# One kernel, two layers, one core: loading the weights in two groups and finishing three of the derived weights inside the main program

## The reference, cut to what matters

```
x_norm = layernorm(x) * norm_g + norm_b
x_proj, z = split(x_norm @ in_proj_W)            # 384 channels each
y_fwd, y_bwd = light_s6(windows of x_proj)       # xproj_W, dt_W, dt_b, A_log, D; 4 steps, 8 states
y_dw  = depthwise 3 x 3 convolution of x_proj    # dw_kernel
y     = alpha * (y_fwd + y_bwd) / 2 + (1 - alpha) * gelu(y_dw @ pw_W)     # alpha = sigmoid(gate)
x_out = x + (y * silu(z)) @ out_W
x     = x_out + gelu((layernorm(x_out) * norm2_g + norm2_b) @ fuse_W1 + fuse_b1) @ fuse_W2 + fuse_b2
```

## Time and profile before

| what | us |
|---|---|
| median of 3 executions | 4724.54 |
| lowest, highest | 4721.48, 4733.52 |
| the profiled execution's own time | 4733.78 |
| its span in the trace | 4732.0 |

### The profile page before, as it was taken

How to read it: one execution, slowest core, us unless ns; L and a number is a source line. 1 busy time by engine, 2 the same in 40 slices (tenths; PEclk the granted TensorE clock), 3 DMA queues, 4 the chain that set the end, 5 groups by cost and what they waited for, 6 DMA issues and landing times. The chain is left out here.

```text
span 4732.0 us, 79417 instructions
## 1 busy us (share of the span) xinstructions
PE 4400.7 (93%) x24320; PEld 3136.2 (66%) x24320; DVE 3875.3 (82%) x7295; ACT 3347.4 (71%) x5828; POOL 3672.9 (78%) x3476
## 2 busy tenths in 40 slices
PE   3799999999999999999998799999999999999998
PEld 2465656565656565656555478877778787878887
DVE  2899999999999999999999477777777777777775
ACT  3888898889898889888986255555555555555555
POOL 1989898989898989989898267766666676666666
PEclk7899999999999999999999799999999999999999
DMA  2011111111111111111111400031001300040000
GB/s 76 12 49 33 49 34 49 33 49 33 49 38 45 38 45 38 44 38 45 40 42 41 129 13 22 21 97 43 22 21 28 105 22 20 22 120 19 16 20 19
DMA packets 139268, 198.15 MB, mean 42 GB/s; under 512 B 18346, under 2 KB 106388, under 8 KB 138644
## 3 DMA queue, kind: packets, MB, share of 16 engines
q1 hardware_dynamic: 138900, 193.76, 12.9%
HBM read 114.02 MB, written 79.69 MB: 41 GB/s over the span
## 5 line engine op out<-in xcount | busy, mean ns | idle before, releaser
L1273 POOL TENSOR_TENSOR pl<-probs,ph 128x512 fp32r<-128x512 f32 x1024 | 1322.2, 1292 | 649.6 <-PE ps_o L1383 322.1
L742 POOL TENSOR_TENSOR dec<-dt,rates 128x384 f32<-128x384 f32 x1536 | 1512.9, 1015 | 285.2 <-ACT dt L628 229.6
L1476 ACT ACTIVATE ph<-ps_s 128x512 fp32r<-128x512 f32 x1024 | 612.7, 598 | 908.3 <-PE ps_s L1366 900.7
L1488 DVE TENSOR_REDUCE part_max<-ps_m 128x1 f32<-128x512 f32 x1024 | 687.4, 688 | 394.4 <-PE ps_m L1349 394.3
L1375 PE MATMUL ps_o<-ph,vh 128*128 128x512 f32 x2048 | 813.4, 397 | 17.6 <-ACT o_ch L1462 17.3
L1375 PE MATMUL ps_o<-ph,vl 128*128 128x512 f32 x2048 | 806.5, 394 | 0.0
L1517 DVE TENSOR_TENSOR ps_a<-probs,ps_a 128x512 f32<-128x512 f32 x992 | 681.3, 687 | 40.8 <-ACT probs L1478 35.3
L1383 PE MATMUL ps_o<-pl,vh 128*128 128x512 f32 x2048 | 635.1, 391 | 0.0
L1478 ACT ACTIVATE probs<-ps_s 128x512 f32<-128x512 f32 x1024 | 607.3, 593 | 0.0
L900 DVE SCALAR_TENSOR_TENSOR psS<-u,bc,psS 128x384 f32<-128x384 f32 x1024 | 597.3, 611 | 1.2
L909 DVE SCALAR_TENSOR_TENSOR y_tok<-psS,bc,y_tok 128x384 f32<-128x384 f32 x960 | 552.3, 604 | 4.5
(11 more groups left out here) (166 smaller groups left out, 7671.8 us busy)
## 6 DMA issues: line engine op xcount, KB each, us to landing
values_d<-hid SPq DMA_DIRECT2D x64, 512.0 KB, 4.3
xf<-in_x_dram SPq DMA_DIRECT2D x128, 128.0 KB
xb<-in_x_dram SPq DMA_DIRECT2D x128, 128.0 KB
residual_d<-xb SPq DMA_DIRECT2D x32, 512.0 KB, 2.6
vh<-values_d SPq DMA_DIRECT2D x32, 512.0 KB, 7.4
vl<-values_d SPq DMA_DIRECT2D x32, 512.0 KB, 9.1
res<-residual_d SPq DMA_DIRECT2D x32, 512.0 KB, 3.3
out_dram<-res SPq DMA_DIRECT2D x128, 128.0 KB
```

The source lines that it names most:

```text
L742: last = nc.gpsimd.tensor_tensor(dec[:, q % RING, j - 1, :], dt[:, par, d, token_of(d, j), :], rates[:, d, n, :], ALU.mult)
L1273: nc.gpsimd.tensor_tensor(pl[:, m % DEPTH, :], probs[:, m % DEPTH, :], ph[:, m % DEPTH, :].bitcast(F32), ALU.subtract).then_inc(pl_ok, 1)
L1476: nc.scalar.activation(ph[:, m % DEPTH, :], ps_s[m % 2][:, :], ACT.Exp).then_inc(ph_ok, 1)
L1488: nc.vector.tensor_reduce(part_max[:, qt, kc:kc + 1], ps_m[r % 2][:, :], AX.X, ALU.max).then_inc(max_out, 1)
```

## The change

The loads of `prepare` are split. The first group of 11 loads counts on `loaded_first`: `in_proj_W`, `Wh`, `Wo`, the two `xproj_W`, and the vectors `norm_g`, `norm_b`, `gate`, `bh`, `fwd_D`, `bwd_D`. After it SP issues the six loads of tile 0's input (`load_front(0)`, moved here from the main program). Then come the other 34 loads on `loaded`, and the two `A_log` tables as before. ACT, PE and DVE start with a wait for `loaded_first`; DVE waits for `loaded` just before the addition of `bo`, three instructions before the end of its list.

The bias rows, `conv_w` and `diag` are no longer made in `prepare`. DVE makes them in `finish_weights`, which the main program calls right after tile 0's `ln1_shift`. PE waits for `bias_ok` before the `dt` matmuls of tile 0 and for `taps_ok` before the parts of its convolution. The raw bias rows lie in `dt` in place of `xb`. Both exponentials of `turn_rates` now wait for both `A_log` tables.

```diff
+            bias_raw = dt[0:66, 0, 0, 0:3, :] ...
@@ main program, DVE
+            def finish_weights():
+                parts = [(bias_row[r0:r0 + 2, 0:n], bias_raw[r0:r0 + 2, 0:n], r0)
+                         for r0, n in ((0, 2 * INNER + C), (64, 2 * INNER))]
+                for row, raw, r0 in parts:
+                    last = nc.vector.tensor_copy(row, raw)
+                last.then_inc(bias_ok, 1)
+                dve.wait_ge(bias_ok, 1)
...
+                last.then_inc(bias_ok, 1)
+                for cb in range(CB):
+                    for tap in range(9):
+                        last = nc.vector.tensor_scalar(conv_w[:, cb, tap, :], eye[:, :], taps[:, cb, tap:tap + 1], None,
+                                                       ALU.mult)
+                for kind in range(2):
+                    for cb in range(CB):
+                        last = nc.vector.tensor_scalar(diag[:, kind, cb, :], ident[:, :], mix[:, 1 + kind, cb:cb + 1],
+                                                       None, ALU.mult)
+                last.then_inc(taps_ok, 1)
...
+                    if tile == 0 and step == "ln1_shift":
+                        finish_weights()
@@ main program, PE
+                    if f == 0:
+                        pe.wait_ge(taps_ok, 1)
...
+                    if f == 0:
+                        pe.wait_ge(bias_ok, 4)
@@ main program, ACT
-                    act.wait_ge(rates_loaded, 16 * (d + 1))
+                    act.wait_ge(rates_loaded, 32)
@@ main program, SP
-            load_front(0)
-            load_back(0)
+            load_back(sp, 0)
@@ prepare, SP
-                for dst, src in loads:
+                for dst, src in loads[:FIRST_LOADS]:
+                    sp.dma_start(dst, src).then_inc(loaded_first, 16)
+                for dst, src in vectors[:FIRST_VECTORS]:
+                    sp.dma_start(dst, src, allow_slow_non_contiguous=True).then_inc(loaded_first, 16)
+                m["load_front"](sp, 0)
+                for dst, src in loads[FIRST_LOADS:]:
                     sp.dma_start(dst, src).then_inc(loaded, 16)
-                for dst, src in vectors:
+                for dst, src in vectors[FIRST_VECTORS:]:
                     sp.dma_start(dst, src, allow_slow_non_contiguous=True).then_inc(loaded, 16)
...
                 sp.wait_ge(loaded, 16 * n_loads)
+                sp.wait_ge(loaded_first, 16 * n_first)
@@ prepare, ACT, PE, DVE
-                act.wait_ge(loaded, 16 * n_loads)
+                act.wait_ge(loaded_first, 16 * n_first)
...
-                pe.wait_ge(loaded, 16 * n_loads)
+                pe.wait_ge(loaded_first, 16 * n_first)
...
-                dve.wait_ge(loaded, 16 * n_loads)
+                dve.wait_ge(loaded_first, 16 * n_first)
...
                 nc.vector.tensor_copy(m["value_w"][:, :, :].rearrange("p b c -> p (b c)"), ps[1][:, :])
 
+                dve.wait_ge(loaded, 16 * n_loads)
                 nc.vector.tensor_tensor(bo_bc, bo_bc, ps[2][:, 0:C], ALU.add).then_inc(dve_ok, 1)
```

More of the change, by code:

```diff
@@ L302, in layer0, with load_front, load_back @@
         rates_loaded = sem("rates_loaded")
+        x_loaded = sem("x_loaded")
+        xb_loaded = sem("xb_loaded")
+        taps_ok = sem("taps_ok")
+        bias_ok = sem("bias_ok")
+        bias_raw = dt[0:66, 0, 0, 0:3, :].rearrange("p t c -> p (t c)")[:, 0:2 * INNER + C]
+        x_tok = x.rearrange("b (j wr dr) (wc dc) c -> (b j) dr dc wr wc c", wr=ROWS // 2, dr=2, dc=2)
+        x_row = x.rearrange("b h w c -> (b h) w c")
+        def load_front(sp, f):
+            for t in range(T):
+                sp.dma_start(xf[:, t, :], x_tok[f, t // 2, t % 2]).then_inc(x_loaded, 16)
+            above = 0 if f == 0 else ROWS * f - 1
+            below = B * H - 1 if f == TILES - 1 else ROWS * f + ROWS
+            sp.dma_start(xf[0:W, T, :], x_row[above]).then_inc(x_loaded, 16)
+            sp.dma_start(xf[W:P, T, :], x_row[below]).then_inc(x_loaded, 16)
+        def load_back(sp, g):
+            for t in range(T):
+                sp.dma_start(xb[:, t, :], x_tok[g, t // 2, t % 2]).then_inc(xb_loaded, 16)
         prepare(nc, w, locals())
@@ L392, in body @@
                         sp.wait_ge(back_full, back_job(g, "x1t1"))
-                        load_back(g + 1)
+                        load_back(sp, g + 1)
                     for i in range(2):
@@ L946, in prepare @@
         loaded = sem("loaded")
+        loaded_first = sem("loaded_first")
         built = sem("built")
@@ L980, in prepare @@
         vectors = []
[L981 to L984 removed]
+        for c, v in ((m["g1_c"], w["norm_g"]), (m["b1_c"], w["norm_b"]), (m["gate_c"], w["gate"]),
+                     (m["bh_c"], w["bh"]), (m["df_c"], w["fwd_D"]), (m["db_c"], w["bwd_D"]),
+                     (m["g2_c"], w["norm2_g"]), (m["b2_c"], w["norm2_b"]), (m["fb1_c"], w["fuse_b1"])):
             vectors.append((col[:, c[0]:c[-1] + 1], channels(v)))
@@ L992, in prepare @@
             vectors.append((m["taps"][:, cb, :], dw[cb]))
-        n_loads = len(loads) + len(vectors)
+        n_first = FIRST_LOADS + FIRST_VECTORS
+        n_loads = len(loads) + len(vectors) - n_first
         with nc.Block() as block:
@@ L1121, in _ @@
                                         ALU.add).then_inc(split_done_dve, 1)
-                dve.wait_ge(split_done_dve, 5)
-                for cb in range(CB):
-                    for tap in range(9):
-                        nc.vector.tensor_scalar(m["conv_w"][:, cb, tap, :], m["eye"][:, :],
-                                                m["taps"][:, cb, tap:tap + 1], None, ALU.mult)
                 dve.wait_ge(act_ok, 1)
```

55 lines of the change are left out of this document (18 added, 37 removed).

## The result

The changed kernel takes 4692.43 us in the median of four executions (4687.49 to 4693.32); the kernel before, run beside it, 4725.72 us (4721.48 to 4733.52). The ratio is 0.9919, with a 95% interval of 0.9905 to 0.9932, which is a gain of 32 to 45 us, 38 by the ratio itself and 33.3 between the medians. Predicted were 4687.3 us and a gain of 37.2. Faster was the right sign, and the time lies in the range of 4680 to 4704. The profiled execution took 4693.32 us where the sum said 4696.6.

The account below looks back on a forecast made before the run. Three idle stretches before tile 0's LayerNorm at 69.03 us were taken to bound the start. 9.2 + 19.3 = 28.5, wait until 30.5, LayerNorm at 31.8: gain 37.2 us, median 4687.3 us, range 4680 to 4704.

Parts of the forecast that it names:

- the sum: Whole profiled execution: 4733.8 us less the 37.2 us gain gives 4696.6 us.
- The first group at 9.2: Start of `prepare`: issuing until about 6.4 us plus 2.7 us landing completes `loaded_first` at 9.2 us.
- DVE's list, 19.3 us, to 28.5: DVE in `prepare`: 19.3 us of remaining work from 9.2 us reaches the addition of `bo` at 28.5 us.
- The wait for `loaded`: Before the addition of `bo`: DVE waits 2.0 us for the taps, until 30.5 us; 33.1 if input data delays them.
- The LayerNorm at 31.8, gain 37.2: Tile 0, main program: input already there, so DVE starts at 31.8 us instead of 69.03, gaining 37.2 us.
- What must hold behind it: Tile 0's front: `A_log` tables, `finish_weights` (12.5 us of DVE) and `load_back(0)` come in time and cost nothing.
- the thinnest margin: `A_log` tables: landed by 38.4 us, wanted by ACT at 41.8, margin 3.4 us.
- The clock in `prepare`: TensorE in `prepare`: 6.4 us of matmuls ran at full clock before; the same clock or better is expected.
- The case of half clock from the first matmul: Rival in `prepare`: DVE reaches the wait 6.4 us later, at 34.9; gain 32.8 us, time 4691.7; chance 0.07.
- Slow entry to the main program: Rival at the block change: entry costs DVE 7.5 us; gain 29.7 us, time 4694.8; chance 0.07.
- Not on the path: Rival for the whole span: a later stage catches up anyway, time stays 4724.5 us; chance 0.05.
- slower: Rival as the pipeline fills: longer half-clock stretch, 80 us costing 71 and giving 4758 us; chance 0.03.

Follow-up runs that it names:

- the late wait: The change, but DVE's wait for `loaded` and what follows it moved into `finish_weights`, and SP no longer waits for `loaded` ending `prepare`; ratio 0.9920.
- the kernel with early rates: The change, but the `A_log` tables load right behind the first group and ACT computes their exponentials in `prepare`; ratio 0.9916.

## Why the prediction was right

*The first group at 9.2.* It came at 9.33, by two errors that cancel: issuing took to 7.22 and not 6.4, because some issues take 0.8 us and not 0.5, and landing took 2.1 us and not 2.7.

*DVE's list, 19.3 us, to 28.5.* It took 18.9, to 28.26. In the two other profiles of the change it took 19.5 and 19.4. What differs is TensorE's clock: the six matmuls that DVE waits for at about 25.6 us take 0.81 us here, at full clock, and 1.28 there and in the kernel before, at half. The wait that follows swallows the difference.

*The wait for `loaded`.* Predicted to end at 30.5 and last 2.0 us; it ended at 30.75 and lasted 2.49. This too is two errors that cancel. SP's issues put the taps 4.46 us later and not 3.66, and they landed 2.15 us after their last issue and not 2.67. Of the bounds, 33.1 (the input's data in the way) did not occur. That this wait, and not DVE, set the end is shown by the late wait, which won 1.6 us at the LayerNorm. It would have won 2.4 (DVE was done 0.8 us before SP) were it not for SP's list: the prediction named one thing behind DVE at this place, and there were two.

*The LayerNorm at 31.8, gain 37.2.* It came at 32.09, gain 36.9. The three parts, each taken back alone, cost 19.5, 12.4 and 9.5 us. These overlap and sum to 41.4. Most of the excess is in the first: without the first group of loads DVE starts at 30.59 and not at 26.81, since the input's issues stand in front of the taps. The rest is in the third, where the input also meets the `A_log` tables. Forward the parts do add up: 17.5 from DVE's start (26.81 to 9.33), 12.4 of work moved, 9.1 from the wait for the input after the block's opening, 0.4 from a list that was shorter in this execution, less the new wait of 2.5, make 36.9.

*What must hold behind it.* `finish_weights` was free, and stayed free with 10.5 us more in it. PE's `dt` came at 58.61 (58.0 predicted), its convolution at 92.1 (91.4). ACT's exponentials started at 42.06 (41.8). The `A_log` tables were there by 40.2 (the second was issued at 29.67 and landed within 10.5 us), not by 38.4, so the thinnest margin was 1.9 us, not 3.4. The small loss from 36.9 at the LayerNorm to 36.55 at the decays lies with PE. The eight matmuls in front of `dt` take 4.63 us where they took 4.27, because the clock comes back to full at 59.93, 5.9 us after they start, and before it came back at 94.74, 3.8 us after. The four `dt` matmuls take 1.55 us and not 0.92, but in the second profile of the change they take 0.92 again and the loss is nearly the same (36.98 us from the LayerNorm to the decays; 37.05 here, 36.66 before).

*The clock in `prepare`.* Here the forecast was right and the reading under it wrong. The prediction took the 1.00 of the first stretches for full clock from the start, and 6.4 us of matmuls at full clock from it. But the trace of the kernel before has no record of a grant before 40.1 us, and that of the change none before 15.6; where no record lies the view shows 1.00. The matmuls themselves tell the clock. PE's timeline after, two groups of the same shape:

```profile
12.52 3.48 PE L1094 MATMUL psF<-hid 128*128 128x256 f32 x8 [1.99 <-DVE hid L1136]
15.83 1.03 PE L1097 MATMUL psF<-hid 128*128 128x256 f32 x4
```

In the trace a matmul starts every 0.43 us up to 15.6 and every 0.21 us from there on, both in stretches shown as 1.00. In the second profile of the change the grant is on record from 17.6, and there the four of L1097 take 1.84 us. The kernel before has the same pair, 3.42 us for eight at 37.20 and 1.03 us for four at 40.46. So PE began at half clock in both kernels, was full for a while, and fell back during the 24 matmuls of one column each (L1104, there L1057). What made it fall there no run shows. DVE's list before had the half clock in it, and "the same clock" was the right forecast. The case of half clock from the first matmul was therefore no rival but what happened each time, and its price of 6.4 us is void: DVE reached the wait at 28.26, not at 34.9. That its 4691.7 us lies close to the time measured is chance. The default that the Trainium skill gives (TensorE: Matmul & The Clock Gate, "Part 1: The HAM clock gate"), throttled until activity releases it, is what the durations of these matmuls show.

*Slow entry to the main program.* This did not occur. DVE was the last to arrive and the first needed, and started at 32.09, 0.04 us after ACT at 32.05. The stall after a taken branch that the Trainium skill describes (Runtime: NRT & Kernel Launch, "Instruction fetch mechanics") is not seen at this change of block in any of the runs; 0.54 us at most lies, at this place, between the last work of one block and the first of the next.

*Not on the path; slower.* What is won at the first decays reaches the end. From first decays to layer 1's loads it was 2547.9 us before and 2546.2 after, and 2541.9 to 2549.2 over all fourteen profiles; from there to the end 2078.4 and 2076.1, and 2075.1 to 2083.4 over all. The kernel before differs from itself by 2.6 us in the first part, and the change by 4.7 in the second. So of the 40.5 us by which the span is shorter, 36.55 are the start and the other 4 are within what one execution differs from the next by. A longer stretch at half clock did not come: 0.78 and 0.99 against 0.77 and 0.99. Its price in the prediction, 0.9 us for each us at half clock, holds for a us of work that is run at half clock; a us spent there loses about 0.5 (an estimate from PE's 94%).

*The time.* 4687.3 predicted, 4692.43 measured. The gain between these medians is 33.3 us; in two further sets it was 36.5 and 33.4, and by the ratio 38. The timeline says 36.55. What is left of the difference, some 3 us, the executions do not resolve.

## What to carry to other kernels

Before a pipeline is full, what counts is the date at which the first long chain starts, and it can be read like a bill: for each engine the first instruction, the wait before it and what ended that wait. Order the loads by who reads them first, and let each consumer wait for its own group only; then put work that only later stages need into an idle gap which the trace already shows, and check the gap by making the work longer. Once loads are reordered, the issuing engine's own list is a term of the sum, both its length and where it must have ended.

## What the runs showed of the hardware

The time of an issue is not a constant. One input load takes 0.53 us of SP's queue in the change and 5.20, 5.01 and 5.22 us in the three kernels in which the two `A_log` tables (1.5 MB each) were issued just before the input. It happens in the change too, where it is hidden: the four issues of `xb`, the next behind the tables, take 5.21 us, and 2.35 in the kernel with early rates, where the tables have long landed. And it happens across queues: with the tables issued by ACT, one of SP's issues took 3.09 us and two 6.53. That the issuer is held up until a backlog has drained fits all of these, but was not tested by itself.

The slower of the two tables lands within 9.5 to 10.6 us when it is issued on SP and up to 16.0 us when it is issued on ACT's queue beside SP's matrices.

TensorE's clock came to full at 40.1 us in the kernel before and at 15.6 after, each time during the same group of matmuls (L1047 and L1094), and fell at 43.5 and 19.0, during the group of one-column matmuls. It followed the work and not the time since the start. It is not the same in every execution: in the three profiles of the change the rise came at 15.6, 17.6 and 17.1 us and the fall at 19.0, 21.0 and 20.5. And a granted clock of 1.00 from the start of a trace to its first record is not evidence of full clock: by the durations of the matmuls PE ran there at half.
